# Gated delta rule: inversion levels on half the columns, side work of the recurrence in a new order

## The reference

```python
qkvz = (x @ W_qkvz)                       # 8 heads, q, k, v, z of 128 each
q, k, v = silu(causal_conv4(q, k, v))
q, k = l2norm(q) / sqrt(128), l2norm(k)   # chunks of 64 tokens from here on
decay = tril(exp(g_i - g_j))              # g: cumulative gate within a chunk
tri = tril((beta * k) @ k.T * decay, -1)
Tm = inverse(I + tri)                     # 64 x 64 per chunk
v_new = Tm @ (beta * v)
k_cum = Tm @ (beta * k * exp(g))
for each chunk:                           # S: state, 128 x 128
    v_n = v_new - k_cum @ S
    out = (q * exp(g)) @ S + tril(q @ k.T * decay) @ v_n
    S = S * exp(g_last) + (k * exp(g_last - g)).T @ v_n
y = (norm(out) * silu(z)) @ W_out
```

## Time and profile before

| | us |
|---|---|
| median of 3 runs | 3494.46 |
| lowest and highest | 3492.59, 3495.26 |
| the profiled execution | 3488.75 |
| its span in the trace | 3487.0 |
| TensorE busy | 3025.8 (87%) |
| DVE busy | 2289.0 (66%) |
| ACT busy | 1233.2 (35%) |
| POOL busy | 1019.2 (29%) |

### The profile page before, as it was taken

The page is one execution under the profiler, slowest core; times in us unless marked ns, Lnnn a source line. Parts: engine busy times, 40 slices in busy tenths (PEclk is TensorE's granted clock), DMA queues, the critical chain, the costliest instruction groups (busy, mean ns, idle before and its releaser), DMA issues. The chain is left out here.

```text
span 3487.0 us, 82116 instructions
## 1 busy us (share of the span) xinstructions
PE 3025.8 (87%) x33083; PEld 2083.1 (60%) x33083; DVE 2289.0 (66%) x5113; ACT 1233.2 (35%) x2979; POOL 1019.2 (29%) x1495
## 2 busy tenths in 40 slices
PE   6999998299966899889889889989989988988597
PEld 3444443166654677667667667667666766766365
DVE  4666666588835675775776666676677667665476
ACT  2333434033323333343343333333334234332354
POOL 3545556057821211212221221221221222121011
PEclk8999999599968999999999999999999999999799
DMA  2111111000001000010010010000000000000000
GB/s 80 32 33 32 34 31 27 30 1 1 1 14 39 23 25 18 17 29 20 17 29 18 19 29 17 20 18 28 20 17 29 20 17 29 17 17 2 25 19 31
DMA packets 94038, 80.40 MB, mean 23 GB/s; under 512 B 54992, under 2 KB 68320, under 8 KB 93664
## 3 DMA queue, kind: packets, MB, share of 16 engines
q1 hardware_dynamic: 93664, 75.18, 7.9%
HBM read 57.70 MB, written 4.85 MB: 18 GB/s over the span
## 5 line engine op out<-in xcount | busy, mean ns | idle before, releaser
L1643 PE MATMUL gd_bk<-gd_xT,gd_wh 128*128 128x512 f32 x768 | 416.0, 653 | 17.1 <-ACT gd_xT L1358 7.8
L1368 ACT COPY gd_O<-gd_bk 64x128 f32<-64x128 f32 x448 | 110.0, 259 | 561.2 <-PE gd_bk L1770 560.8
L1413 DVE SCALAR_TENSOR_TENSOR gd_YK<-gd_bk,gd_cw,gd_YK 128x511 f32<-128x511 f32 (+2 forms) x384 | 285.5, 743 | 18.5 <-ACT gd_YK L1290 11.9
L390 DVE TENSOR_REDUCE at_nm<-at_ring 128x2 f32<-128x256 f32 (+3 forms) x256 | 199.2, 820 | 145.9 <-PE at_ring L531 145.9
L1471 DVE COPY_PREDICATED gd_U<-gd_mU,gd_bk 128x256 f32<-128x256 int32 x320 | 140.9, 440 | 201.1 <-PE gd_bk L1836 138.3
L1379 ACT COPY gd_ZS<-gd_bk 128x256 f32<-128x256 f32 x320 | 119.1, 372 | 387.3 <-PE gd_bk L1814 379.6
L1814 PE MATMUL gd_bk<-gd_L,gd_NT 64*64 64x64 f32 x5120 | 203.7, 223 | 57.8 <-DVE gd_L L1473 57.8
L1814 PEld LDWEIGHTS gd_bk<-gd_L,gd_NT 64*64 64x64 f32 x5120 | 169.2, 134 | 112.5 <-DVE gd_L L1473 75.2
L1831 PE MATMUL gd_bk<-gd_U,gd_ZS 64*64 64x64 f32 x5120 | 203.4, 221 | 0.1
L276 POOL TENSOR_TENSOR at_PT<-at_PT,at_dm 128x1024 f32<-128x1024 f32 (+3 forms) x128 | 197.3, 1541 | 10.6
L1786 PE MATMUL gd_bk<-gd_V,gd_KK 64*128 64x128 f32 x896 | 165.8, 306 | 38.6 <-DVE gd_V L1564 38.2
(11 more groups left out here) (358 smaller groups left out, 6746.4 us busy)
## 6 DMA issues: line engine op xcount, KB each, us to landing
gd_wh<-in_L_attn_W_qkvz SPq DMA_DIRECT2D x64, 512.0 KB, 3.7
gd_gb<-gates SPq DMA_DIRECT2D x128, 64.0 KB, 3.3
X<-in_L_attn_x SPq DMA_DIRECT2D x8, 512.0 KB, 8.7
at_QT<-at_QS SPq DMA_DIRECT2D x128, 32.0 KB, 1.9
at_KT<-at_KS SPq DMA_DIRECT2D x128, 32.0 KB, 1.9
at_OC<-at_Ob SPq DMA_DIRECT2D x128, 32.0 KB, 1.9
at_RC<-inverse SPq DMA_DIRECT2D x128, 32.0 KB, 1.8
out_x<-X SPq DMA_DIRECT2D x8, 512.0 KB, 2.9
```

Of the source, the lines that this page charges most:

```text
L390: nc.vector.tensor_reduce(nm[v % 2][:, k, c0:c0 + HS + 1:HS], set_of(s, 2 + p)[:, :, 0:n], AX.X, ALU.max).then_inc(max_done, 1)
L1413: nc.vector.scalar_tensor_tensor(out[:, s:W], bank_[:, 0:W - s], cw[:, j, head(f, e), CONVK - 1 - s:CONVK - s], out[:, s:W], ALU.mult, ALU ...
L1643: ins = nc.tensor.matmul(out[:, :], wh[e][:, k, col * DK:(col + 1) * DK], xT[:, k, :], start=k == 0, stop=k == DC - 1)
```

## The change

First, each level works on the columns that it changes. At level l, of each 2 x 2^l columns only the half that is written is computed and copied. The moving operand of each product is that half (32 of 64 columns per chunk), the result stands packed in the bank, and the copies of ACT and DVE read it packed and write it to every other block. The masks become real tiles of 128 x 4 x 64 in place of broadcast ones. ZS is zeroed once by POOL, so that its other half is zero at the first use; its untouched columns are multiplied too. The number of matmuls and their stationary operands stay as they are.

```diff
-        mU = [sb(f"mU{l}", [P, CK], I32) for l in range(LEVELS)]
+        mU = [sb(f"mU{l}", [P, TPS, CK], I32) for l in range(LEVELS)]
...
+        def side(ap, l, bit):
+
+            return ap.rearrange("p (b s n) -> p b s n", s=2, n=1 << l)[:, :, bit, :]
...
+        def packed_rows(b_, part, c, t, l):
+
+            return b_[rows(c), part * TPS * HC + t * HC:part * TPS * HC + (t + 1) * HC].rearrange("p (b n) -> p b n", n=1 << l)
...
+                for e in E2:
+                    nc.gpsimd.memset(ZS[e][:, :, :], 0.0).then_inc(zs_zero[e], 1)
...
-                                nc.scalar.copy(ZS[e][:, :, :], chunks(A_[e])).then_inc(zs_done[e], 1)
+                                nc.scalar.copy(side_all(ZS[e], l, 0), packed(A_[e], 0, l)).then_inc(zs_done[e], 1)
...
-                    last = nc.vector.copy_predicated(U[e][:, :, :], wide(mU[l]), chunks(A_[e], 1))
+                    last = nc.vector.copy_predicated(side_all(U[e], l, 1), side_mask(mU[l], l, 1), packed(A_[e], 2, l))
...
-                                        last = nc.tensor.matmul(A_[e][rows(c), t * CK:(t + 1) * CK], NTm[e][rows(c), t, :], L[e][rows(c), t, :],
-                                                                start=True, stop=True)
+                                        last = nc.tensor.matmul(packed_rows(A_[e], 0, c, t, l), NTm[e][rows(c), t, :],
+                                                                side(L[e][rows(c), t, :], l, 0), start=True, stop=True)
...
-                                        last = nc.tensor.matmul(A_[e][rows(c), (TPS + t) * CK:(TPS + t + 1) * CK], ZS[e][rows(c), t, :],
-                                                                U[e][rows(c), t, :], start=True, stop=True)
+                                        last = nc.tensor.matmul(packed_rows(A_[e], 2, c, t, l), ZS[e][rows(c), t, :],
+                                                                side(U[e][rows(c), t, :], l, 1), start=True, stop=True)
```

More of the change, by code:

```diff
@@ L1345, in front @@
                         keys_first(f, 0)
+                        keys_first(f, 1)
                     if n == 1:
[L1347 to L1353, removed]
+                        keys_out(f, 0)
+                    if n == 2:
+                        gate_out(f, 0)
+                    if n == 3:
+                        keys_out(f, 1)
+                        gate_out(f, 1)
+                    if n in (5, 6):
+                        values_first(f, n - 5)
+                    if n == 8:
+                        queries_first(f, 0)
                 decays(0, 0)
@@ L1384, in _ @@
                                 decays(f + 1, 1)
[L1385 removed]
+                            values_out(f, 0)
                         if l == 2 and has(f):
[L1387 removed]
                             values_out(f, 1)
@@ L1391, in _ @@
                             heads_out(q, 1)
+                        if l == 3 and has(f):
+                            queries_out(f, 0)
                         if l == 4 and has(f):
-                            queries_out(f, 0)
                             queries_out(f, 1)
@@ L1598, in _ @@
                             for s in range(1, CONVK):
-                                values_tap(f, 0, s)
+                                values_tap(f, 1, s)
                         if l == 2 and has(f):
                             for s in range(1, CONVK):
-                                values_tap(f, 1, s)
+                                queries_tap(f, 0, s)
                         if l == 3 and has(f):
-                            for s in range(1, CONVK):
-                                queries_tap(f, 0, s)
-                        if l == 4 and has(f):
                             for s in range(1, CONVK):
@@ L1710, in lower_across @@
                         for c in range(CPT):
-                            last = nc.tensor.matmul(F1[e][rows(c), t * CK:(t + 1) * CK], NTm[e][rows(c), t, :], identc[rows(c), :],
+                            last = nc.tensor.matmul(packed_rows(F1[e], 0, c, t, 0), NTm[e][rows(c), t, :], side(identc[rows(c), :], 0, 0),
                                                     start=True, stop=True)
@@ L1803, in _ @@
                                 last.then_inc(oi_mm[e], 1)
-                    if has(f):
-                        queries_in(f, 0)
                     for l in range(1, LEVELS):
@@ L1835, in _ @@
                                         for c in range(CPT):
-                                            last = nc.tensor.matmul(A_[e][rows(c), t * CK:(t + 1) * CK], U[e][rows(c), t, :], ZS[e][rows(c), t, :],
-                                                                    start=True, stop=True)
+                                            last = nc.tensor.matmul(packed_rows(A_[e], 1, c, t, l), U[e][rows(c), t, :],
+                                                                    side(ZS[e][rows(c), t, :], l, 0), start=True, stop=True)
                                 last.then_inc(y_mm[e], 1)
```

111 lines of the change are left out of this document (68 added, 43 removed).

## The result

The changed kernel takes 3630.39 us (median, 3625.89 to 3631.73) against 3493.53 us for the kernel before on the same chip: ratio 1.0393, 95% interval 1.0375 to 1.0411. It is slower by 137 us. Forecast were 3361 us and a range from 3290 to 3440.

The account below looks back on a forecast made before the run. TensorE, busy 87% of the span, was taken as the bound. Per pair: steps -5.9 us, columns -0.4, levels 0, clock 1.7 given back, hand-offs +0.3; net -4.3, over 31 pairs -133, giving 3361 us; range 3290 to 3440.

Parts of the forecast that it names:

- What bounds the kernel: Whole kernel: TensorE, busy 87% of the span; steps and levels mostly its throughput, the rest waits that can be named.
- the steps: Recurrence steps up to the levels' first product: the new order cuts 35.84 to 29.9 us, 5.9 us a pair.
- rival 2: Recurrence steps: DVE becomes the bound and 2.1 us a pair is given back, 3426 us; chance 0.20.
- The stall in level 2: Level 2: TensorE idles 1.95 us waiting for ACT's ZS copy, queued behind silu of values 0 and table loads.
- The copies: Levels: half the elements save DVE about 0.14 us a copy, 2.5 us a pair, only part on the path.
- The columns: TensorE's level products: 32 moving columns take 27 ns an instruction, saving 1.0 us of work, 0.4 on the path.
- the upper rows: Profile rows on matmul groups: the longer of weights and moving side sets the time, so 64-column weights keep it.
- Rival 1: Levels: moving columns alone set TensorE's time, groups take 0.23 us, 6.4 us a pair, 3296 us; chance 0.12.
- floor of about 25 ns between starts: Level products: by that rule alone groups go from 29 to 25 ns, 1.8 us a pair, sum some 20 us lower.
- The clock: Pair loop: 1.7 us a pair given back, worth one 3.4 us stretch at half clock, because of the level 2 stall.
- Rival 3: Levels: TensorE's clock falls after the 2 us stall, 3.3 us a pair slower, 3597 us; chance 0.08.
- today's pair recovers after one stretch: Argument against the falling clock in the levels: the old pair held one 3.4 us stretch at half clock, then recovered.

Follow-up runs that it names:

- kernel 1: Changed kernel's new order of side work, with products and copies of the levels put back to all 64 columns; 3402.61 us, ratio 0.9722.
- 5: kernel 1 with the silu of values 0 moved behind the ZS copies of level 2 on ACT; 3355.7 us, ratio 0.9596.
- kernel 6: Changed kernel with products on 64 columns, half copies and the level 2 stall kept; 3363.35 us, ratio 0.9614.
- kernel 4: kernel 3 with products on 64 columns and half copies read from the unpacked bank; 3316.89 us, ratio 0.9481.
- 10: Kernel before the change, old order of side work and wide products, with half copies added; 3462.2 us, ratio 0.99.
- kernel 3: Changed kernel with the silu of values 0 moved behind the ZS copies of level 2 on ACT; 3503.19 us, ratio 1.0015.
- kernel 2: Kernel before the change, old order of side work kept, with the levels on 32 columns; 3674.94 us, ratio 1.0511.

## Why the prediction was wrong

**What bounds the kernel, and the steps: right.** The levels were to begin 29.9 us after the first key projection and begin after 29.87. On average over the 31 pairs the steps fall from 35.84 to 30.26 us, 5.6 where 5.9 was forecast. The waits of the key transposes are gone, queries_in(0) starts at 27.47 (forecast 27.4) behind the 0.45 us wait for DVE's first level, and DVE did not become the bound (21.2 of 29.9 us), so rival 2 falls.

**The stall in level 2: right in place, too long.** 1.95 us was forecast; 1.43 us is there in the pair shown, 1.29 on average. Kernels 1 and 5, and 6 and 4, price it at 1.5 us per pair behind wide products.

**The copies: right in the later levels only.** DVE was to save 0.14 us a copy at all levels. DVE in order of time in the changed kernel, a copy of level 1 and one of level 2:

```profile
2083.86 0.45 DVE L1502 COPY_PREDICATED gd_U<-gd_mU,gd_bk 128x128 f32<-128x128 int32 x1 [0.20 <-PE gd_bk L1876]
2084.10 0.49 DVE L1504 COPY_PREDICATED gd_L<-gd_mL,gd_bk 128x128 f32<-128x128 int32 x1
...
2088.84 0.29 DVE L1502 COPY_PREDICATED gd_U<-gd_mU,gd_bk 128x128 f32<-128x128 int32 x1 [1.23 <-PE gd_bk L1876]
2089.04 0.28 DVE L1504 COPY_PREDICATED gd_L<-gd_mL,gd_bk 128x128 f32<-128x128 int32 x1
```

From level 2 on 0.15 us is saved; in level 1, in blocks of two floats, and in the first level, in single ones, nothing. The mean over levels 1 to 5 is 0.33 us against 0.44, so 0.11 is saved. Even so the copies bring 35 to 39 us in three pairs of kernels, and 19 to 29 us of that are the shorter waits for L named under 6 and 10.

**The columns: the step that failed.** The prediction's term was "1.0 us of work, and of it 0.4 us on the path", with the bounds "0 and 6.5 us of work", both gains, under the sentence "A slower group than now I exclude". At full clock that sentence holds and the upper rows decided rightly: 0.46 us a group, next to no gain, against 0.47, and 0.2 us a pair (kernels 3 and 4). Rival 1 falls with it. The Trainium skill's floor of about 25 ns between starts (TensorE: Matmul & The Clock Gate, section "Wait — 56ns, not 53.3ns?") did not bind either: 0.46 us are 29 ns an instruction. (By the prediction's own share on the path the 1.8 us of work that it worked out from that floor would have been worth 10 us in the sum, not 20.) What was left out is that a group's time is not its only effect. With all groups narrow the granted clock was 0.51 for 23.9 us, although TensorE's rows are busy for 100% of them. In place of -0.4 us a pair stands 267 us over 31 pairs (kernel 6 to the changed kernel), +8.6 us a pair. Without this term the rest of the sum comes out well: kernel 6, with wide products, takes 3363 us, and the forecast less its 0.4 us a pair is 3374. Part of that agreement is luck. In kernel 6 the steps gain 5.4 us on average, not 5.9, and the rest of the pair loses 1.3, not the 2.0 that the other terms add up to.

**The clock: named, and given too little.** The sum's own term for it was the 1.7 us given back for one stretch of 3.4 us at half clock a pair; measured are 22.4 us a pair. Rival 3 was this outcome, at its price of 3597 against 3630 measured, with a chance of 0.08 and outside the range. Its trigger was the stall, and that is half of the story. The stall does bring the clock down behind wide products too, in 12 and 11 of 31 pairs (kernels 1 and 6), but for 3.4 us only, and the clock over the loop stays at 0.98 and 0.99. Behind narrow products every pair falls with the stall, for 13.7 us or more, and 21 or 28 of 31 without it (kernels 3 and 2). The argument against the rival, "today's pair recovers after one stretch", was taken from a kernel whose levels move 64 columns. That is just what the change took away: kernel 1 recovers within the same levels, while the changed kernel comes back only within the last products (2108.2 to 2116.4, which move 64 and 128 columns) or in the output projection. The Trainium skill (same page, section "The HAM clock gate") says that recent activity releases the clock, and it was right to make that a rival here. That TensorE is busy without a gap did not settle it, as the stretch at 0.51 shows.

**The sum.** In the pair shown: steps -5.97 us, behind the steps +10.3, net +4.3. In the forecast the same two terms were -5.9 and, with the clock given back, +1.6. That 31 times 4.3 is near the 137 us measured is partly luck of the pair. On average over the 31 pairs the steps give -5.6 and the rest +9.5, net +3.9 or 121 us. The first pair, which has narrow levels but no recurrence to win time in, adds 9.6 us, and some 6 us outside the loop are not placed.

What stays open: why 3 pairs in kernel 2 and 10 in kernel 3 are spared, and whether some wait, however short, must come first. The long stretches at half clock in kernels 2 and 3 all begin within a pair's levels, and in the one pair of each that was looked at in order of time behind a wait for L of about 0.8 us; no kernel was run that has narrow products and no wait at all.

## What to carry to other kernels

Before a matmul is narrowed, ask what its weights cost: with 64 columns of weights, 32 moving columns took as long as 64 (0.46 us a group against 0.47), so next to nothing was gained, and the clock was lost. Keep redundant columns in the products and cut them in the copies, where ACT and DVE do get faster; here that alone turned 4% slower into 4% faster (kernel 6), and 5% with the stall gone (kernel 4). And read a kernel's tolerance of waits as belonging to its present instructions: a stall of some 40 us in all cost 47 us behind wide products and 127 us behind narrow ones.

## What the runs showed of the hardware that was not expected

TensorE was issued matmuls without a gap for 23.9 us and granted 1.2 GHz throughout (0.51 in the table of stretches), in levels whose groups move 32 columns against 64 of weights. With 64 moving columns the same order of work was granted 0.98 to 1.00. With only 10 or 18 of the 28 groups narrow the levels stayed at full clock in all but one pair. Narrow groups alone do not rule out full clock either: they ran at it in 10 pairs of kernel 3 and behind the output projection of the changed kernel.

At half clock such a group takes 0.85 us, 53 ns an instruction. The Trainium skill (TensorE: Matmul & The Clock Gate, section "LDWEIGHTS (loading the stationary operand)") gives the columns of the weights over 1.2, in ns, for a load. For 64 columns that is 53 ns, an estimate from the page's figure. The starts at half clock are as far apart, but at full clock the rows show 29 ns, so they do not confirm it as what sets the time.

DVE's masked copy of 128 floats per partition takes 0.44 to 0.49 us in blocks of one or two floats and 0.28 to 0.30 in blocks of four and more; 256 in one run took 0.44. ACT's copy of the same halves takes 0.264 us on average at all levels, against 0.372.
